# Two quarters of the product with the values issued together in every second step of the self-attention

## The reference

```python
# 16 heads of 16 columns, 4 key/value heads, so 4 query heads share one key/value head
q, k, v = xn @ Wq + bq, xn @ Wk + bk, xn @ Wv + bv       # xn: layernorm of x
scores = einsum('bghnd,bhsd->bghns', q, k)               # 4 batches x 4 kv heads x 4 heads, 1024 x 1024
attn = softmax(scores / sqrt(16), axis=-1)
out = einsum('bghns,bhsd->bghnd', attn, v)
x = x + out @ Wo + bo
```

## Time and profile before

| what | value |
|---|---|
| median of 3 runs | 2142.9 us (2128.15 to 2145.97) |
| time of the profiled execution | 2110.68 us |
| its span | 2109.1 us |
| granted TensorE clock, mean of the span | 0.913 of full speed |
| TensorE busy (matmul) | 1825.4 us, 87% |
| VectorE busy | 1265.4 us, 60% |
| ScalarE busy | 1072.1 us, 51% |
| self-attention, first to last step with pass B | about 158 to 848 us of the span |

### The profile page before, as it was taken

How to read it: one execution, slowest core, us unless ns; L and a number is a source line. 1 busy time by engine, 2 the same in 40 slices (tenths; PEclk the granted TensorE clock), 3 DMA queues, 4 the chain that set the end, 5 groups by cost and what they waited for, 6 DMA issues and landing times. The chain is left out here.

```text
span 2109.1 us, 36974 instructions
## 1 busy us (share of the span) xinstructions
PE 1825.4 (87%) x11908; PEld 1183.2 (56%) x11909; DVE 1265.4 (60%) x2019; ACT 1072.1 (51%) x2750; POOL 332.4 (16%) x443
## 2 busy tenths in 40 slices
PE   7699999999999999889899999630849999999676
PEld 3333333333333333579789999520737888888465
DVE  6497999999999980332589999440352222222254
ACT  2206888888888887112478888500242333323121
POOL 3000000000000000400122222147020111111254
PEclk9857999999999998878999999865979999999898
DMA  5651211121112000342001100142521111111343
GB/s 166 167 181 31 40 25 25 34 40 25 25 33 40 25 3 2 107 146 97 5 6 53 52 4 4 66 169 103 180 75 43 50 50 52 50 50 50 133 129 107
DMA packets 91253, 139.21 MB, mean 66 GB/s; under 512 B 19164, under 2 KB 64656, under 8 KB 89616
## 3 DMA queue, kind: packets, MB, share of 16 engines
q1 hardware_dynamic: 78128, 101.75, 16.8%
q0 software_dynamic: 11920, 35.66, 5.1%
q10 hardware_dynamic: 1104, 0.43, 0.1%
HBM read 73.51 MB, written 53.81 MB: 60 GB/s over the span
## 5 line engine op out<-in xcount | busy, mean ns | idle before, releaser
L493 DVE TENSOR_REDUCE neg_max<-psA 128x1 f32<-128x1024 f32 x512 | 623.4, 1223 | 74.3 <-PE psA L538 71.1
L519 ACT ACTIVATE PT<-psB 128x512 f32<-128x512 f32 x1024 | 552.4, 597 | 166.3 <-PE psB L550 147.2
L538 PE MATMUL psA<-KS,QS 48*128 48x512 f32 x1024 | 397.2, 472 | 31.0 <-PEq L101 16.0
L550 PE MATMUL psB<-QS,KS 50*128 50x512 f32 x1024 | 392.6, 459 | 17.4 <-ACT PT L519 17.4
L567 PE MATMUL psO<-PT,VG 128*32 128x256 f32 x4096 | 337.1, 403 | 0.0
L538 PEld LDWEIGHTS psA<-KS,QS 48*128 48x128 f32 x1024 | 162.0, 198 | 257.7 <-DVE neg_max L493 196.8
L567 PEld LDWEIGHTS psO<-PT,VG 128*32 128x32 f32 x4096 | 82.4, 109 | 188.8 <-issue 108.5
L550 PEld LDWEIGHTS psB<-QS,KS 50*128 50x128 f32 x1024 | 158.0, 190 | 51.7 <-ACT PT L519 50.3
L1878 DVE TENSOR_TENSOR m_xT<-m_psT,m_xT 128x256 fp32r<-128x256 f32 x72 | 30.6, 425 | 249.0 <-ACT m_xT L1920 249.0
L1325 ACT ACTIVATE x_probs<-x_scores,x_neg_max 128x77 f32<-128x77 f32 x512 | 176.3, 358 | 4.0 <-DVE x_neg_max L1231 3.9
L1175 PE MATMUL psYx<-VO,x_ET 128*128 (+1 forms) x640 | 146.0, 383 | 1.4 <-ACT x_ET L1348 0.9
(11 more groups left out here) (201 smaller groups left out, 2834.9 us busy)
## 6 DMA issues: line engine op xcount, KB each, us to landing
QS<-q_parts SPq DMA_DIRECT2D x96, 128.0 KB
xs<-zero_row POOLq DMA_DIRECT2D x1, 9216.0 KB, 33.6
m_x<-xs SPq DMA_DIRECT2D x72, 128.0 KB
ys<-m_y POOLq DMA_DIRECT2D x72, 128.0 KB, 2.0
q_parts<-part SPq DMA_DIRECT2D x16, 512.0 KB, 2.7
OT<-OU SPq DMA_DIRECT2D x32, 256.0 KB, 2.6
KS<-k_parts SPq DMA_DIRECT2D x32, 128.0 KB
WG<-in_Wg SPq DMA_DIRECT2D x8, 512.0 KB
```

What stands on the lines that cost most here:

```text
L493: dve.tensor_reduce(neg_max[:, e, col:col + 1], psA[:, v % 2, :, :].rearrange("p a n -> p (a n)"), axis=AX.X, op=ALU.max, negate=True).the ...
L519: act.activation(PT[:, k % 4, 2 * a + r, :], psB[:, bank_of(slot, 2 * u + a), :], ACT.Exp, scale=SCALE).then_inc(exp_done, 1)
L538: mm = pe.matmul(psA[:, v % 2, n, :], QS[top:top + KQ, slot, a, t * P:(t + 1) * P], KS[top:top + KQ, slot, n * HALF:(n + 1) * HALF], start ...
L550: pe.matmul(psB[:, bank_of(slot, m), :], KS[top:top + KM, slot, c * P:(c + 1) * P], QS[top:top + KM, slot, a, half * HALF:(half + 1) * HAL ...
```

## The change

The quarters of the product with the values are no longer issued one at the end of each step. An even step issues pass A and pass B only. An odd step issues them and then two quarters one after the other, the one that the even step had and its own. The 1024-wide maxima and the written-out loops are as before. Each quarter has the same instructions, operands and semaphore waits as before, and the order of the quarters is the same; the four quarters after the last group are issued as before.

```diff
@@ -586,10 +586,13 @@
                             pass_a(i + ahead, (slot + ahead) % SLOTS, (u + LEAD) % NU, n)
                         pass_b(i, slot, u, n)
 
-                    if u >= LAG:
-                        times_values(i, e, u - LAG)
-                    elif not (isinstance(i, int) and i < 1):
-                        times_values(i - 1, 1 - e, u - LAG + NU)
+                    if u % 2 == 0:
+                        continue
+                    for w in (u - LAG - 1, u - LAG):
+                        if w >= 0:
+                            times_values(i, e, w)
+                        elif not (isinstance(i, int) and i < 1):
+                            times_values(i - 1, 1 - e, w + NU)
```

## The result

| | before | after |
|---|---|---|
| median of 4 runs | 2135.5 us (2124.9 to 2146.0) | 2175.8 us (2173.2 to 2178.6) |
| profiled execution, span | 2109.1 us | 2173.8 us |
| mean granted clock in its span | 0.913 | 0.896 |

The ratio is 1.0189, 95% interval 1.0126 to 1.0252: 40 us slower. 2182 had been forecast. The agreement is better than the reasoning behind it, as the traces show.

The account below looks back on a forecast made before the run. TensorE's order bounds the kernel before; afterwards pass B's ring of three adds a wait. Plain pairs +51, half clock -2, psO copies -1 and group starts -9 make +39 us on the median 2142.9: 2182 us, range 2153 to 2217.

Parts of the forecast that it names:

- What bounds the kernel: Before the change, TensorE's own order sets the step of 1.23 us; VectorE's ceiling is 4% away.
- The quarters: Two quarters in a row in the odd step take 1.00 us, against 1.14 apart; the upper end is 1.14.
- The ring: Pass B's fourth matmul waits for the first one's bank until 1.25 us, 0.25 late; the pair becomes 2.67, 0.21 more.
- The start of the odd step: Pass B's four matmuls in a pair would start at 0, 0.33, 0.67 and 1.00 us without the wait.
- the first rival: Drain only: fourth matmul finds its bank free, TensorE needs 2.33 us a pair, VectorE binds at 2.42; 2133 us; 6%.
- The exponentials: On ScalarE, one takes about 0.60 us alone and they follow each other at 0.49, from four in 2.26 us.
- Copies and group starts: Stalls at the copies of psO change by -1 us over 32, waits at group starts by -9 us over 15.
- The start at half clock: At half clock the ring doesn't bind; the dozen pairs there, at start and end, gain about 0.15 each: -2 us.
- The clock falls: Rival: TensorE streams less, so its clock drops; +11 us per fall of 29 us; from 2200 us up; 5%.
- its own sign: Wrong if the fourth matmul starts by 1.0, quarters cost much over 1.0, or half clock appears between 210 and 783 us.

Follow-up runs that it names:

- ring3_narrow: Changed kernel with both pass A matmuls of a unit written to one 512-wide bank, so the maxima leave out half the keys; three banks for pass B; 2075.3 us.
- half_exp_after: Changed kernel with each exponential over only 256 of its 512 columns, PT filled with ones at the start; full maxima, three banks; 2004.7 us.
- ring4_narrow: Four banks for pass B in place of three, against ring3_narrow, with the maxima again leaving out half of the keys; 1911.9 us.
- the corners: Table of all thirteen traces by fourth matmul's wait and copy's stall: 8 or 9 short clock falls where both occur, 0 in the others.
- before_again: The kernel before, unchanged, run and traced again on another chip; 2120.8 us, ratio 1.016 against itself.
- the second set: Follow-up runs sharing one chip; there the changed kernel, run again, took 2089.0 us against 2027.6 for the kernel before, ratio 1.033.
- after_all: Changed kernel with later psO copies, maxima turned after unit 2 and unread pass A matmuls in the last 42 steps; 2104.3 us, 1.005 of the kernel before.

## Why the prediction was right, and where it wasn't

**What bounds the kernel.** Right for the changed kernel: `ring3_narrow` halves the maxima and the pair stays at 2.68. For the kernel before, whose maxima run without a gap, the forecast read TensorE as the bound from the steps without pass A; no run tried it with shorter maxima, and the 2.46 to which VectorE holds `half_exp_after` is as long as its pair. So in the kernel before VectorE's limit lies too close behind TensorE's for the rows to tell them apart.

**The quarters.** Right: two in a row take 1.00 us (413.39 to 414.39), the value taken from the half-clock rows, where 1.14 was the other end. The second quarter is 0.14 cheaper than one apart. That the change of tiling is what costs the 0.14 is the forecast's reading; no run tests it.

**The ring.** Right, to 0.01 us: 1.25, 0.43, 1.00. `ring4_narrow` shows it as cause, by removing the wait.

**The start of the odd step.** Wrong: I gave all matmuls of the pair a distance of 0.33, and steps that follow each other without a quarter have 0.24. The third started at 0.57, not 0.67, the fourth's turn came at 0.80, not 1.00, and it was 0.45 late, not 0.25. The wait hid the error: the order saves TensorE 0.33 us a pair (2.46 to 2.13), not 0.14, and the ring takes 0.55 back, not 0.34, and these leave nearly the same difference. It shows in the first rival's 2.33 for TensorE, which is 2.13; VectorE then holds the pair at 2.46, as `half_exp_after` shows, where I had 2.42.

**The exponentials.** The distance of 0.49 is right but doesn't come out of the row given for it, since four in 2.26 us leave 0.55; six in 3.04 behind the copy do give 0.49.

**Copies and group starts.** Right: -1.4 and -8.4 us against -1 and -9, and the pair with the copy 3.68 against 3.66. The start at half clock gave -8, not -2, since the clock rose at 167 us and not at 187. The rise came between 155 and 171 us in all eight traces with the changed order of the quarters, and between 172 and 202 in all five with the old one. So these 8 us seem to belong to the change too, by a way that the forecast didn't have and no run was made for.

**The clock.** This is the term that was missed. "The clock falls" stood as a rival with 5% and from 2200 us; it came true in its short form in every trace of the changed kernel, for 19 us, and the last group's stretch for another 18. The argument against it, that the steady clock is 1.00 through all of today's stalls, holds for one stall at a time, as the corners show. The forecast called itself wrong if half clock appeared between 210 and 783 us; it did, eight times, so on the clock it failed by its own sign though its time fits.

**Why the number still fitted.** In part by luck. The forecast put 39 us on the median of before; the traces differ by 65 in their spans and 74 in the phase. The trace of before was a favourable execution (2110.7 against a median of 2135.5, with 7 us of half clock in the last group), and `before_again` shows one place where executions of this kernel differ: 22 us there. So the timed runs of before probably held clock losses that its trace didn't, and these stood against the 37 us that the forecast lacked; they have no traces to show it. Even the 38 us without those rows meet the 39 by two misses that cancel, +56 for +51 in the plain pairs and -8 for -2 at the start. On the chip of the second set, where the kernel before varied between 2001 and 2040, the change cost 61. What the order itself costs, about 40 us net, is what `after_all` shows. How the remainder of a given chip's difference divides between the clocks of the two kernels is known only for the traced executions.

Still open are what precisely tips the clock when both stalls meet, and why it rises sooner after the start with the changed order. Whether work that serves no result, put into the fourth matmul's wait, would keep the clock wasn't tried.

## What to carry to other kernels

Batching like work on an in-order engine empties the other engines' slots into bursts: count the longest run of producers between two batches against the ring that they share, here four matmuls into three banks, and price the wait from the consumer's start and length. The batch saved TensorE 0.33 us a pair here (0.14 at the quarters, 0.19 at the matmuls of pass B that now follow each other) and cost 0.55 since the ring is one short (0.45 us late and 0.10 for starting alone). And before reading a stall's price as its length, look at the granted clock on both sides of it: two waits that each left the clock alone cost more together than their sum, and a repair as cheap as moving the copies by one step in ScalarE's order was worth 45 us to the kernel before, about as much as the change under study cost.

## What the runs showed of the hardware

- In the last group of the changed kernel the clock stood at 1.2 GHz for 78 us, with TensorE busy 51.5 of 56 us, and matmuls that serve no result, on the other 64 rows, kept it at 2.4. `ring4_narrow` kept 2.4 there without them. Matmuls of the same kind beside the first group's pass A raised nothing: half clock until 202 us.
- A matmul of pass B or A follows its like at 0.24 us where its forerunner's weights were loaded ahead (414.01, 414.24 in `ring4_narrow`). Behind one that starts with its own weight load it follows at 0.33, be it the first behind the quarters (413.68, 414.01) or one released late by VectorE in `half_exp_after` (410.47, 410.81). The quarters follow a fourth matmul that starts alone at 0.43.
- The part of the program behind the phase took some 90 us less on two chips than on the two others (1162 to 1166 us against 1251 to 1257), for every kernel; its cause wasn't found.
